# Which queue loads the first projection's weights: SyncE's, second in line, or ScalarE's, first in line

## What is computed

```python
xx = jnp.pad(x, ((0, 0), (1, 0), (0, 0)))[:, :-1]      # the position before
xk = x * time_mix_k + xx * (1.0 - time_mix_k)          # xv, xr alike
k = jnp.einsum('btc,dc->btd', xk, Wk)                  # v from xv, Wv
sr = jax.nn.sigmoid(jnp.einsum('btc,dc->btd', xr, Wr))
rwkv = sr * _wkv(w, time_first, k, v)                  # recurrence over positions
x = _layernorm(x + jnp.einsum('btc,dc->btd', rwkv, Wo))
h = jax.nn.silu(gate) * up                             # gate, up: x with int weights / 127
x = _layernorm(x + jnp.einsum('bsh,dh->bsd', h, wd))
```

## Time and profile before

| | us |
|---|---|
| median of 3 runs | 291.11 |
| lowest and highest | 290.76, 291.33 |
| profiled execution, device time | 291.55 |
| profiled execution, span of the profile | 289.7 |
| TensorE busy with matmuls in the span | 273.9 (95%) |
| VectorE busy | 261.1 (90%) |
| ScalarE busy | 214.9 (74%) |
| GpSimd busy | 191.6 (66%) |

### The profile page before, as it was taken

The page is one execution under the profiler, slowest core; times in us unless marked ns, Lnnn a source line. Parts: engine busy times, 40 slices in busy tenths (PEclk is TensorE's granted clock), DMA queues, the critical chain, the costliest instruction groups (busy, mean ns, idle before and its releaser), DMA issues.

```text
span 289.7 us, 4280 instructions
## 1 busy us (share of the span) xinstructions
PE 273.9 (95%) x1258; PEld 199.1 (69%) x1258; DVE 261.1 (90%) x451; ACT 214.9 (74%) x388; POOL 191.6 (66%) x155
## 2 busy tenths in 40 slices
PE   7999978889999999999999999999999999999990
PEld 5754565646794689648885679568965789778890
DVE  4996599899999999999999999999899999889773
ACT  3488797489667987699966986798858892799473
POOL 3638699979968875986768675986566580334051
PEclk9999999999999999999999999999999999999998
DMA  7900600220103102230204010210211020102003
GB/s 236 374 6 12 209 1 0 73 72 3 36 2 80 67 0 72 47 100 0 72 5 144 1 54 19 72 36 0 72 29 44 1 75 0 36 2 74 0 3 113
DMA packets 13541, 16.26 MB, mean 56 GB/s; under 512 B 720, under 2 KB 11216, under 8 KB 13520
## 3 DMA queue, kind: packets, MB, share of 16 engines
q1 hardware_dynamic: 12832, 15.48, 16.7%
q10 hardware_dynamic: 688, 0.53, 0.6%
HBM read 11.81 MB, written 4.19 MB: 55 GB/s over the span
## 4 chain that ended last, share of the span: by engine, by line
PE 72%; DVE 11%; ACT 8%; issue 4%; DMA 1%; POOL 1%; SPq 0%; DVEq 0%; POOLq 0%; ACTq 0%
PE bank_b L1163 12%; PE bank_a L1163 12%; PE bank_a L1186 11%; PE bank_b L1119 9%; PE bank_a L1082 7%; PE bank_c L1082 7%; PE bank_d L1082 7%; PE bank_b L1140 2%; DMA wkT<-wk 1%; DVE rwkv L786 1%; DVE state L746 1%; ACT L606 1%; POOL hlo L405 1%; PE bank_d L1109 1%; ACT wts L492 1%
## 5 line engine op out<-in xcount | busy, mean ns | idle before, releaser
L405 POOL TENSOR_TENSOR hlo<-hid,hhi 128x512 fp32r<-128x512 f32 (+1 forms) x37 | 54.0, 1466 | 31.7 <-ACT hhi L584 31.6
L378 POOL TENSOR_SCALAR wts<-gap,par 128x512 f32<-128x512 f32 (+1 forms) x18 | 35.9, 1995 | 24.4 <-DVE gap L714 23.5
L500 ACT ACTIVATE mix<-dx,par 128x512 f32<-128x512 f32 x48 | 31.4, 712 | 19.0 <-POOL dx L358 19.0
L1186 PE MATMUL bank_a<-wd_r,hhi 128*128 128x256 f32 x180 | 44.2, 287 | 1.0 <-POOL hlo L405 0.9
L1186 PE MATMUL bank_a<-wd_r,hlo 128*128 128x256 f32 x180 | 42.8, 279 | 0.0
L364 POOL TENSOR_TENSOR mix<-mix,xt 128x512 f32<-128x512 f32 (+1 forms) x36 | 40.7, 1164 | 0.3 <-ACT mix L500 0.3
L1186 PEld LDWEIGHTS bank_a<-wd_r,hhi 128*128 128x128 f32 x180 | 33.8, 188 | 3.5 <-issue 2.6
L1186 PEld LDWEIGHTS bank_a<-wd_r,hlo 128*128 128x128 f32 x180 | 33.8, 188 | 0.3 <-issue 0.2
L862 DVE TENSOR_TENSOR hid<-bank_b,act 128x512 f32<-128x512 f32 (+1 forms) x48 | 30.8, 643 | 3.6 <-issue 1.1
L584 ACT ACTIVATE hhi<-hid 128x512 fp32r<-128x512 f32 (+1 forms) x53 | 30.6, 579 | 4.4 <-DVE hid L862 4.4
L492 ACT ACTIVATE wts<-wts 128x512 f32<-128x512 f32 (+1 forms) x54 | 27.9, 577 | 7.5 <-DVE wts L723 7.3
(11 more groups left out here) (129 smaller groups left out, 598.1 us busy)
## 6 DMA issues: line engine op xcount, KB each, us to landing
xrow<-x SPq DMA_DIRECT2D x7, 512.0 KB, 3.8
xt<-xT SPq DMA_DIRECT2D x6, 513.0 KB, 3.7
out<-y_buf SPq DMA_DIRECT2D x6, 512.0 KB, 2.9
wg_i<-wg SPq DMA_DIRECT2D x1, 768.0 KB, 7.7
wu_i<-wu SPq DMA_DIRECT2D x1, 768.0 KB, 9.1
wd_i<-wd SPq DMA_DIRECT2D x1, 768.0 KB, 10.7
out<-y_buf SPq DMA_DIRECT2D x3, 256.0 KB, 2.2
xt<-xT SPq DMA_DIRECT2D x2, 257.0 KB, 2.9
```

What stands on the lines that cost most here:

```text
L378: nc.gpsimd.tensor_scalar(wts[:, OUT, h, 0:n], gap[:, h, 0:n], par[:, FIRST, h:h + 1], CAP, ALU.add, ALU.min).then_inc(out_arg_ready, 1)
L405: nc.gpsimd.tensor_tensor(hlo[:, m, 0:n], hid[:, m % NH, 0:n], hhi[:, m, 0:n].bitcast(f32), ALU.subtract).then_inc(hlo_ready, 1)
L500: nc.scalar.activation(mix[:, s, i, h, 0:n], dx[:, h, 0:n], ACT.Copy, scale=par[:, MIX + i, h:h + 1]).then_inc(dx_scaled, 1)
L1186: mm = nc.tensor.matmul(ffn[:, q, :], hp.bitcast(f32) if full else hp, w[:, m, :], start=(m == 0 and q % 2 == 0 and part is hhi), stop=(m ...
```

## The change

The load of wkT is taken out of SyncE's list, where it was second, and put at the head of ScalarE's, ahead of par. Nothing else is changed.

```diff
             sp.dma_start(xt0[:, :, :], xT_v[:, :, 0:steps(0) + 1]).then_inc(xt0_in, 16)
-            sp.dma_start(wkT[:, :, :], wk.rearrange("(h p) d -> p h d", p=P)).then_inc(wk_in, 16)
             load_xt(1)
...
+            nc.scalar.dma_start(wkT[:, :, :], wk.rearrange("(h p) d -> p h d", p=P)).then_inc(wk_in, 16)
             nc.scalar.dma_start(par[:, :, :], params).then_inc(par_in, 16)
             nc.scalar.dma_start(wvT[:, :, :], wv.rearrange("(h p) d -> p h d", p=P)).then_inc(wv_in, 16)
             nc.scalar.dma_start(wrT[:, :, :], wr.rearrange("(h p) d -> p h d", p=P)).then_inc(wr_in, 16)
```

## The result

The changed kernel takes 294.64 us (median of 6 runs, 294.38 to 295.24) against 291.22 us (6 runs, 290.76 to 291.65) of the kernel before: a ratio of 1.0119 with a 95% interval of 1.0106 to 1.0132. It is 3.4 us slower. The direction was forecast, the size was not: 294.64 lies far above the range, which ended at 292.8.

A forecast was written before the change was run, and what follows sets the result against it. TensorE, fed by wkT with VectorE's mix right behind, was taken to bound the start; a 0.6 us wrT stall containing 0.1 us from terms 1 and 2 gave 291.7 to 292.15, forecast at the middle, 291.9 us; range 290.8 to 292.8.

The forecast's parts named there:

- The reading of what bounds the start: Start-up chain: wkT's transfer, then TensorE unbroken to 31.0 us; VectorE's mix next limit; shifts before 31 us count one for one.
- Term 1: wkT earlier: issued at 0.75 instead of 1.25 us, landing at 4.85; third k pass gains at most 0.09 us.
- Term 2: xt0 and par later: xt0 by 0.15 us (0 to 0.5), par delaying VectorE by 0.2 us (0 to 0.7).
- Term 3: wvT, third on ScalarE's queue, lands at 7.7 us (5.5 to 7.9), wanted by TensorE at 7.97; cost zero.
- Term 4: wrT, fourth on ScalarE's queue, lands at 10.3 us (8.4 to 11.4), wanted at 9.70; TensorE stalls 0.6 us (0 to 1.7).
- The rival of the slower pace: TensorE's clock steps up later after longer idle time; 8 slower passes cost 1.7 us, hiding wrT's stall: 292.8; chance 0.09.
- The other two rivals: wrT in time, 290.9 to 291.5, chance 0.34; VectorE's half 1 mix 0.35 us shorter, time 290.7, chance 0.07.
- The structure of the sum: At TensorE's r projection, wrT's 0.6 us stall contains the 0.1 us of terms 1 and 2, rather than adding to it.

## Why the prediction was wrong, by its own steps

- **The reading of what bounds the start** held: VectorE's mix stood right behind wkT, and the delay went through TensorE's closed stretch one for one (2.89 us at r's weights, 3.0 at the end).
- **Term 1** held. wkT landed at 4.8, as worked out, and could give nothing.
- **Term 2 is the step that failed**, in size. par was taken at 4.6 us (4.43 + 0.2) with an upper end of 5.1, wkT's landing "and then some tenths more". It landed at 6.2: 1.4 us behind wkT. The rule that queues take turns by packets had been applied to wrT and not to par, whose 128 packets are half as many as the 256 of a 256 KB load of weights, each turn beside a 2 KB row. Holding those rows back brought par to 5.0. xt0 was off too: 4.5 us, taken at 4.0 with 4.35 as the limit. VectorE's second mix came 1.8 us late where 0.2 was taken and 0.7 allowed, and TensorE's third pass with it.
- **Term 3** was mis-sized: wvT landed at 9.2, taken at 7.7, upper end 7.9. The 517 KB up to its end were counted as equal to wrT's old position, but xt's 2 KB rows now came up a slot earlier beside it; with SyncE's later loads held back wvT landed at 5.6.
- **Term 4**, called the deciding one, had the right mechanism, and 11.8 us where 10.3 was taken and 11.4 allowed. The step from wvT to wrT was right, 2.6 us as estimated (the division as given, 256 by 103, makes it 2.5): from 9 to 10 us q10 sent 95 packets beside 94 on q1, 0.10 MB beside 0.29. The miss is term 3's, carried on. By itself it is a floor worth 2.1 us at r's weights (11.77 against 9.70) and 2.5 in the medians (293.51 against 291.04 beside it), where 0.6 was taken. In the changed kernel the forecast wait for wrT doesn't show, because VectorE and the clock keep TensorE back to 12.6.
- **The rival of the slower pace** came true, but not as written and not instead of the others. It had the step up come later; in the trace the clock was up and fell after the idle time. It named par and xt0 as what could make the idle time, but priced the clock alone (1.7 us, hence 292.8), as an alternative with a chance of 0.09; the delay that makes the idle time comes on top. Its price in the trace was 1.07 us; alone in the kernel before a later rise cost 1.45.
- **The other two rivals** fell: wrT was not in time, and VectorE's second mix took 0.85 us as before, beside GpSimd's work from 6.93 us on.
- **The structure of the sum** was right: two parallel paths of which the later one counts. But it had the wrong one as the later. par, VectorE and the clock reach to 12.6 us, 1.82 + 1.07 = 2.89 us late where 0.1 was taken for terms 1 and 2; the late weights reach to 11.8 to 12.05. Taking away par's lateness gave 1.2 us, taking away the clock's 0.8, both together 1.1; only when the weights were in time too did the time return to 291.5. The direction was right, by a wait that the changed kernel doesn't have.

## What to carry to other kernels

A small load that everything waits for goes ahead of bulk loads on its queue; its cost is counted in packets and not in bytes, against the rows of the other queue. When a start-up load is moved, work out anew the landing of every load on both queues, since taking one off a queue lets long rows come up earlier beside the other. When TensorE gets a new idle stretch, price the clock after it as well, on top of the delay that made the idle time.

## What had not been expected of the hardware

- Moving a 5 KB load from ScalarE's queue to SyncE's moved the landing of a 256 KB load by 2.7 us (11.7 to 9.0), with the same weights in the same order on ScalarE's queue, issued some 0.4 us earlier.
- par needed 4.9 us for 5 KB where it had needed 2.4.
- The kernel before has slower executions of its own: 12 of 13 runs on one chip lay from 290.64 to 291.85, and one at 293.66. None of these was traced, so that the clock makes them isn't shown.
- The granted clock in the stretches of the kernel before (columns as in the earlier trace rows) reads 1.00 from the start on, though the passes up to 7.3 us are at the lower pace:

```profile
0.00:5.00 5.00, 3.77 (x8) 2.52 (x8) 1.35 (x8) 1.99 (x3) 0.76 (x7) 1.00 0.57 174
5.00:8.30 3.30, 2.91 (x10) 2.35 (x10) 3.02 (x6) 0.51 (x1) 1.57 (x2) 1.00 1.04 383
```

  With SyncE waiting for par it also reads 1.00 while passes are 0.43 us apart up to 10 us. The column showed the fall in the changed kernel, but no late rise; there only the spacing of the passes tells it.
